# Gated mixing on two images at a time with full-width loads, and the squares moved into a forward transform whose image blocks are stationary

## The chip, the cores and the metric

One core of a Trainium2 chip runs the whole program. The metric is the device time of one execution in microseconds (us). The engines are named as the profile names them: PE is TensorE (PEld its weight loads), DVE is VectorE, ACT is ScalarE, POOL is GpSimd, SP is SyncE, which here only issues transfers. Weights stay in PE ("stationary") while the other operand streams through ("moving"). All data are float32.

## The reference, cut to what matters

The input x has 8 images, 64 channels and 256 x 256 pixels. Two layers follow each other. `_gn` normalises groups of two channels of one image.

```python
x = x + _L0_conv_ref(_gn(x), ...)     # gated mixing
x = x + _L1_conv_ref(_gn(x), ...)     # spectral layer

# layer 0, u = _gn(x), per image
y   = einsum('bwhc,dc->bwhd', u, mlp1_w) + mlp1_b
x1  = _shift1(y[..., :c]);  x2 = _shift2(y[..., c:2*c])   # quarters of the channels move by one pixel, edges repeated
x3  = sigmoid(batchnorm(u) * wbn) * u
out = bar0 * x1 + bar1 * x2          # bar from a small softmax of the pooled sums
o   = einsum('bwhc,dc->bwhd', out, mlp2_w) + mlp2_b
return o * x3

# layer 1, u = _gn(x), 64 channels in and out, m1 = m2 = 32
x_ft = rfft2(u)
out_ft[:, :, :m1, :m2]  = einsum('bixy,ioxy->boxy', x_ft[:, :, :m1, :m2],  w1)
out_ft[:, :, -m1:, :m2] = einsum('bixy,ioxy->boxy', x_ft[:, :, -m1:, :m2], w2)
return irfft2(out_ft)
```

Layer 0 comes down to four 64 x 64 matrices per image, one for each direction of shift, applied to shifted copies of x. The result is multiplied by a gate and added to x. The value that the kernel calls x1 (not the one above) is the output of layer 0.

## The kernel before

The program is a row of stages with a barrier between them. Only the third to the fifth change.

1. Statistics: x is read once in full-width tiles, DVE takes means and variances.
2. Small matrices: `wall` (the four 64 x 64 matrices of each image) and `params` (gate scale, bias, mean, offset).
3. **Gated mixing** (L511 to L740). The work is cut into 128 blocks. A block is 16 rows of one image: its upper 8 rows lie with 64 channels on partitions 0 to 63, its lower 8 rows on partitions 64 to 127, in the tile `mix_x` whose rows are W + 1 = 257 numbers long. SP loads each half with a transfer of its own (L564, L567; 9 rows of 64 channels, pieces of 1 KB). Each half must also hold the other copy, moved by one row and one column, because the matmuls take both tap pairs from one tile at a contraction of 128. So DVE copies 64 partitions up (L686) and 64 down (L691). POOL then fills the edge column with two multiplies by one, 64 partitions x 17 numbers each (L589). PE does 16 matmuls of 64 output columns and 512 moving columns (L617), two tap pairs accumulated; the two row parities write to PSUM partitions 0 to 63 and 64 to 127 and run side by side. ACT subtracts the mean (L640, in two halves of 64 partitions, in every second block one half of it on DVE, L699), takes the sigmoid (L648), issues the store (L661) and squares the output with a sum (L666). DVE adds the offset and multiplies by the gate (L721, one operand in PSUM), then adds 1, multiplies by the centred x and sums (L730, two operands in SBUF). In each turn DVE prepares block n + 2 while PE is on block n + 1. The order of each engine is written by hand: loops of 32 blocks, waits on counting semaphores.
4. A short stage between: table loads, then the second normalisation's mean and variance for all images from `sums` and `sqs` (L740 to L797).
5. **Forward transform** (L800 to L1080). x1 is read back in groups of 8 channels, image rows on the partitions. DVE adds and POOL subtracts the two halves of the image (L1007, L1077), PE transforms along the rows with the table `frow` as the stationary operand (L869, 64 output columns for the even and 64 for the odd frequencies, side by side, 512 moving), ACT evacuates (L983), PE transposes (L880), DVE evacuates (L1052) into `fwd_cols`, and PE transforms the other direction (L901) in five parts of up to 16 matmuls. The factor `ncur` of the normalisation is applied when ACT (L965) and DVE (L1023) copy the parts out.
6. Mixing of the modes, then the inverse transform, the addition of x1 and the output. These stay, but for the address from which x1 is read.

## Time and profile before

| | us |
|---|---|
| median of 3 runs | 3113.48 |
| lowest, highest | 3108.65, 3118.16 |
| the profiled execution, in all | 3114.35 |
| its span (first to last instruction) | 3112.7 |
| statistics and small matrices | 0 to 378.6 of the span |
| gated mixing and its drain | 378.6 to 1464.9 |
| second normalisation's stage | 1464.9 to 1471.9 |
| forward transform | 1471.9 to 2093.5 |
| modes, inverse, output | 2093.5 to 3112.7 |

The rows shown further down give for a group of instructions the line, the engine, the shapes, the count, the busy time and the mean of one instruction, and how long the engine was idle just before them and who ended that. A matmul in float32 has two records, so 16 matmuls are 32 records. A timeline row has a start in us from the beginning of the span and a duration.

### The profile page before, as it was taken

Reading aid. Unit: us, or ns where it says so; the run is one execution under the profiler, and the core shown is the slowest. Engines: PE = TensorE matmul, PEld = TensorE weight load, DVE = VectorE, ACT = ScalarE, POOL = GpSimd, SP = SyncE. Lnnn points to the kernel's source line nnn. Section 1 sums busy time; section 2 is a strip of 40 time slices with the busy share of each in tenths; the row PEclk is TensorE's granted clock in tenths of the full one; section 3 lists DMA queues with packets and bytes.
Section 4 is the critical chain, followed back from the end, with each engine's and each line's share of the span. In section 5 each row is a group of like instructions: output and inputs, shape, how many; then the busy total and the mean of one; then the engine's idle time right before and its main releaser. Section 6 shows DMA issues by size and latency. Waiting matters only on the chain. (4 is left out here: it accounts for less than half of the span.)

```text
span 3112.7 us, 38323 instructions
## 1 busy us (share of the span) xinstructions
PE 2255.8 (72%) x12960; PEld 1076.6 (35%) x12960; DVE 2025.2 (65%) x2317; ACT 1302.1 (42%) x1470; POOL 757.3 (24%) x477
## 2 busy tenths in 40 slices
PE   0000288888889889896899898965555989988884
PEld 0000123222223223232345444534555444444442
DVE  8999689989999999997665555640000454544442
ACT  1111078878887888886332222310001222212220
POOL 1000023222323232322655454510000111111111
PEclk9999899999999999998999999987888999998987
DMA  9999299999999999997877676739999999999999
GB/s 402 428 428 428 70 254 264 269 249 276 269 267 257 273 275 267 270 271 215 346 258 260 238 259 243 258 95 347 355 342 317 362 384 395 394 378 409 401 376 351
DMA packets 456398, 949.63 MB, mean 305 GB/s; under 512 B 16608, under 2 KB 377744, under 8 KB 410928
## 3 DMA queue, kind: packets, MB, share of 16 engines
q1 hardware_dynamic: 250720, 619.62, 61.8%
q10 hardware_dynamic: 169984, 192.95, 19.5%
q0 software_dynamic: 35536, 134.84, 11.5%
q8 instruction: 113, 1.85, 0.2%
q14 instruction: 45, 0.37, 0.0%
HBM read 653.75 MB, written 293.60 MB: 304 GB/s over the span
## 5 line engine op out<-in xcount | busy, mean ns | idle before, releaser
L617 PE MATMUL psum<-mix_x,wcur 128*64 128x512 f32 x4096 | 938.1, 614 | 148.6 <-POOL mix_x L589 137.4
L617 PEld LDWEIGHTS psum<-mix_x,wcur 128*64 128x64 f32 x4096 | 311.9, 139 | 774.2 <-issue 564.8
L1227 PE MATMUL psum<-tab_irow_icol_sign,inv_t 128*128 128x512 f32 x1024 | 497.0, 609 | 15.7 <-DVE weights_or_rows L1322 15.1
L589 POOL TENSOR_TENSOR mix_x<-mix_x,one 64x17 f32<-64x17 f32 x256 | 324.0, 1266 | 745.6 <-DVE mix_x L691 738.1
L640 ACT ACTIVATE centred<-mix_x,pcur 64x2048 f32<-64x2048 f32 x192 | 384.2, 2001 | 205.2 <-POOL mix_x L589 188.5
L1322 DVE TENSOR_TENSOR weights_or_rows<-weights_or_rows,psum 128x1024 f32<-128x1024 f32 x224 | 272.7, 1221 | 265.7 <-PE psum L1227 228.5
L983 ACT ACTIVATE fwd_rows<-psum 128x512 f32<-128x512 f32 x256 | 152.2, 598 | 414.6 <-PE psum L869 384.8
L730 DVE SCALAR_TENSOR_TENSOR mix_out<-gated,centred 128x2048 f32<-128x2048 f32 x128 | 293.6, 2294 | 39.4 <-issue 35.2
L264 DVE BATCH_NORM_STATS2 stats<-stat_x 128x6 f32<-128x512 f32 x512 | 305.4, 676 | 13.4 <-DMA stat_x<-x 13.0
L721 DVE SCALAR_TENSOR_TENSOR gated<-psum,pcur,gated 128x2048 f32<-128x2048 f32 x128 | 300.9, 2351 | 18.0 <-PE psum L617 16.4
L1052 DVE COPY fwd_cols<-psum 128x136 f32<-128x136 f32 x512 | 154.6, 394 | 237.8 <-PE psum L880 236.7
L869 PE MATMUL psum<-fwd_sum,tab_ident_frow_fcol 128*64 128x512 f32 x512 | 282.5, 635 | 28.4 <-POOL fwd_diff L1077 18.5
L1291 ACT ACTIVATE inv_t<-psum 128x256 f32<-128x256 f32 x256 | 98.4, 384 | 477.3 <-PE psum L1218 477.3
L869 PE MATMUL psum<-fwd_diff,tab_ident_frow_fcol 128*64 128x512 f32 x512 | 282.8, 636 | 0.0
L1077 POOL TENSOR_TENSOR fwd_diff<-fwd_x 128x2048 f32<-128x2048 f32 x48 | 224.3, 4673 | 239.1 <-PE psum L869 205.6
L648 ACT ACTIVATE gated<-centred,pcur 128x2048 f32<-128x2048 f32 x128 | 268.2, 2095 | 9.6 <-DVE centred L699 1.8
L1202 PE MATMUL psum<-weights_or_rows,modes_or_terms 128*16 128x64 f32 x4096 | 170.3, 354 | 135.3 <-DMA modes_or_terms<-modes_in 111.8
L1227 PEld LDWEIGHTS psum<-tab_irow_icol_sign,inv_t 128*128 128x128 f32 x1024 | 199.5, 196 | 164.8 <-issue 146.1
L666 ACT ACTIVATE square<-mix_out 128x2048 f32<-128x2048 f32 x128 | 242.4, 1894 | 3.6 <-DVE mix_out L730 3.6
L296 PE MATMUL psum<-s_ones_dmask_spread_npix,w1d 128*64 128x128 f32 x1 | 0.4, 396 | 333.7 <-PEq L200 333.7
L1218 PE MATMUL psum<-tab_irow_icol_sign,modes_or_terms 128*128 128x256 f32 x512 | 159.7, 396 | 97.1 <-ACT modes_or_terms L1285 97.1
L1334 POOL DMA_DIRECT2D out<-weights_or_rows x112 | 98.7, 886 | 463.6 <-DMA out<-weights_or_rows 229.3
(185 smaller groups left out, 1982.4 us busy)
## 6 DMA issues: line engine op xcount, KB each, us to landing
mix_x<-x SPq DMA_DIRECT2D x240, 576.0 KB, 8.0
stat_x<-x SPq DMA_DIRECT2D x64, 2048.0 KB, 13.0
x_scratch<-mix_out ACTq DMA_DIRECT2D x128, 1024.0 KB, 9.1
weights_or_rows<-x_scratch SPq DMA_DIRECT2D x112, 1024.0 KB, 10.9
out<-weights_or_rows POOLq DMA_DIRECT2D x112, 1024.0 KB, 16.5
fwd_x<-x_scratch SPq DMA_DIRECT2D x96, 1024.0 KB, 6.8
x_tile<-x_scratch SPq DMA_DIRECT2D x46, 1024.0 KB, 8.0
weights_or_rows<-L_conv_w_real SPq DMA_DIRECT2D x8, 4096.0 KB, 34.3
```

What stands on the lines that cost most here:

```text
L264: last = nc.vector.bn_stats(stats[:, at:at + 6], XT[t % NX][:, q * 512:(q + 1) * 512])
L589: last = nc.gpsimd.tensor_tensor(XT[n % NX][h, :, to], XT[n % NX][h, :, of], one[h, :], ALU.mult)
L617: last = nc.tensor.matmul(bank(k * 4 + q, 512, C, par * C), wcur[j][:, m * C:(m + 1) * C], XT[n % NX][:, r0:r0 + 3:2, m:m + W], start=(m = ...
L640: last = nc.scalar.activation(XC[n % NX][h, :].rearrange("p (r w) -> p r w", w=W), XT[n % NX][h, 1:MR:2, 1 - half:1 - half + W], ACT.Ident ...
L648: nc.scalar.activation(G[n % NX][:, :], XC[n % NX][:, :], ACT.Sigmoid, bias=pcur[j][:, 1:2], scale=pcur[j][:, 0:1]).then_inc(sig_done, 1)
L666: nc.scalar.activation(SQ[:, :], XO[k][:, :], ACT.Square, accum_out=sqs[:, bass.ds(i * NI + n, 1)]).then_inc(sq_done, 1)
L721: nc.vector.scalar_tensor_tensor(out=G[n % NX][:, :], in0=psum[:, k * SC:(k + 1) * SC], scalar=pcur[j][:, 3:4], in1=G[n % NX][:, :], op0=A ...
L730: nc.vector.scalar_tensor_tensor(out=XO[k][:, :], in0=G[n % NX][:, :], scalar=1.0, in1=XC[n % NX][:, :], op0=ALU.add, op1=ALU.mult, accum_ ...
L869: last = nc.tensor.matmul(bank(n % 2, 512, C, par * C), frow[:, par, :], ED[G0 % 2][par][:, 2 * cp:2 * cp + 2, :], start=True, stop=True)
L1077: nc.gpsimd.tensor_tensor(ED[G0 % 2][1][:, :, :], XW[G0 % NX][:, 0, :, :], XW[G0 % NX][:, 1, :, :], ALU.subtract).then_inc(diff_done, 1)
L1227: last = nc.tensor.matmul(bank(n % 2 * 2 + a), TS[n % 2][:, a * P:(a + 1) * P], icol, start=True, stop=True)
L1322: nc.vector.tensor_tensor(xw, xw, psum[:, n % 2 * 1024:n % 2 * 1024 + 1024] .rearrange("p (a k) -> p a k", a=2), ALU.add).then_inc(added, 1)
```

## The change

The mixing now takes a pair of images: the first image's 64 channels on partitions 0 to 63, the second's on 64 to 127, 8 rows a block, again 128 blocks. One transfer of 10 rows and 128 partitions fills the tile `mix_u` (U; rows of 258 numbers, six buffers). A second tile `mix_v` (V, four buffers) takes the copies: image 0's matmuls read U, image 1's read V. The sixteen matmuls keep their shape; the two images take the places of the two row parities. The loops are written out.

- POOL pads both edge columns in one instruction of 128 x 20 numbers and copies 64 partitions x 2321 numbers from U to V ("up").
- ACT copies 64 x 2322 numbers from U to V ("low"), subtracts the mean on 128 partitions, takes the sigmoid; it squares nothing here.
- DVE copies 64 x 2321 numbers inside U ("double"); both multiply steps stay, the second writes over the gate's tile, from which the store is issued (four buffers instead of two).

```diff
-            NX = 4
-            XT = [sb(ph, f"mix_x{i}", [P, MR + 1, PITCH]) for i in range(NX)]
+            NU, NV = 6, 4
+            U = [sb(ph, f"mix_u{i}", [P, OWN * PITCH]) for i in range(NU)]
+            V = [sb(ph, f"mix_v{i}", [P, TAPS * PITCH]) for i in range(NV)]
...
+                        if n >= NU:
+                            sp.wait_ge(conv_done, n - NU + 1)
...
+                        sp.dma_start(u[:, lo - r0:hi - r0, 1:W + 1],
+                                     x_rows[pair, lo:hi, :]).then_inc(loaded[n % NU], 16)
...
+                    def pad(n):
+                        pool.wait_ge(loaded[n % NU], loaded_by(n))
+                        if n >= 2:
+                            pool.wait_ge(up_done, n - 1)
...
+                    def up(n):
+                        pool.wait_ge(padded, min(n + 2, NI))
+                        if n >= NV:
+                            pool.wait_ge(conv_done, n - NV + 1)
+                        k = TAPS * PITCH - 1
+                        nc.gpsimd.tensor_copy(V[n % NV][C:P, 0:k], U[n % NU][C:P, SHIFT:SHIFT + k]).then_inc(up_done, 1)
...
+                    def low(n):
...
+                        nc.scalar.activation(V[n % NV][0:C, 0:k], U[n % NU][C:P, 0:k], ACT.Copy).then_inc(low_done, 1)
...
-                            nc.scalar.activation(SQ[:, :], XO[k][:, :], ACT.Square,
-                                                 accum_out=sqs[:, bass.ds(i * NI + n, 1)]).then_inc(sq_done, 1)
...
+                        nc.vector.tensor_copy(U[n % NU][C:P, 0:k], U[n % NU][0:C, SHIFT:SHIFT + k]).then_inc(doubled, 1)
```

The order on DVE in the middle of the mixing, before: one turn makes the upper copy of block n + 2, multiplies block n, makes the lower copy, multiplies again, and in every second turn subtracts a mean.

```order
L686 COPY mix_x3<-mix_x3 64x8x256 [waits mix_loaded3]
L719 REGISTER_ALU
L721 SCALAR_TENSOR_TENSOR gated1<-psum,pcur0,gated1 128x2048 [waits mix_sig,mix_conv]
L691 COPY mix_x3<-mix_x3 64x8x256
L727 REGISTER_ALU
L729 REGISTER_ALU [waits mix_stored1,mix_h]
L730 ISA [waits mix_sq]
L730 SCALAR_TENSOR_TENSOR mix_out1,sums<-gated1,centred1 128x2048
L699 TENSOR_SCALAR centred3<-mix_x3,pcur0 64x2048 [waits mix_doubled]
```

And in the changed kernel, two turns:

```order
L702 SCALAR_TENSOR_TENSOR gated1<-psum,pcur0,gated1 128x2048 [waits mix_sig,mix_conv]
L690 COPY mix_u3<-mix_u3 64x2321 [waits mix_v_up,mix_v_low,mix_xc]
L709 SCALAR_TENSOR_TENSOR gated1,sums<-gated1,centred1 128x2048 [waits mix_h]
L702 SCALAR_TENSOR_TENSOR gated2<-psum,pcur0,gated2 128x2048 [waits mix_sig,mix_conv]
L690 COPY mix_u4<-mix_u4 64x2321 [waits mix_v_up,mix_v_low,mix_xc]
L709 SCALAR_TENSOR_TENSOR gated2,sums<-gated2,centred2 128x2048 [waits mix_h]
```

A turn has lost one copy and the mean; the copy that is left waits for ACT's and POOL's copies instead of for the load.

POOL at the same place, before:

```order
L589 TENSOR_TENSOR mix_x0<-mix_x0,one 64x17 [waits mix_doubled]
L589 TENSOR_TENSOR mix_x0<-mix_x0,one 64x17
L586 REGISTER_ALU
L589 TENSOR_TENSOR mix_x1<-mix_x1,one 64x17 [waits mix_doubled]
L589 TENSOR_TENSOR mix_x1<-mix_x1,one 64x17
```

and in the changed kernel:

```order
L578 TENSOR_TENSOR mix_u0<-mix_u0,one 128x10x2 [waits mix_v_up,mix_loaded0]
L587 COPY mix_v1<-mix_u5 64x2321 [waits mix_conv,mix_padded]
L578 TENSOR_TENSOR mix_u1<-mix_u1,one 128x10x2 [waits mix_v_up,mix_loaded1]
L587 COPY mix_v2<-mix_u0 64x2321 [waits mix_conv,mix_padded]
L578 TENSOR_TENSOR mix_u2<-mix_u2,one 128x10x2 [waits mix_v_up,mix_loaded2]
```

The pad has moved from behind DVE's last copy to ahead of it, right behind the load, and a large copy has come to POOL.

The forward stage has no sums and differences, no transposes and nothing on POOL. A block of x1 (128 image rows x 128 columns of one channel) is the stationary operand and a table of 128 columns (33 cosines and 33 sines, each in a field of 34) is the moving one, so the result is already transposed. ACT squares each tile there with a sum, in four instructions of 128 x 1024. The second normalisation's stage is gone: the means are made at the start of the forward stage, the variance of an image when its last tile is squared (a copy `spread`, one matmul of one column, a root, two reciprocals).

```diff
-                        for par in range(2):
-                            last = nc.tensor.matmul(bank(n % 2, 512, C, par * C), frow[:, par, :],
-                                                    ED[G0 % 2][par][:, 2 * cp:2 * cp + 2, :],
-                                                    start=True, stop=True)
...
+                        for k in range(RC):
+                            for s in range(2):
+                                at = n % 2 * 1024 + k * 256 + s * P
+                                for a in range(2):
+                                    last = nc.tensor.matmul(psum[:, at:at + P],
+                                                            XW[t % NX][:, a, c0 + k, s * P:(s + 1) * P],
+                                                            frow[:, a, :], start=(a == 0), stop=(a == 1))
...
+                            nc.scalar.activation(junk[g % 2][:, :, :],
+                                                 XW[t % NX][:, :, 2 * g:2 * g + 2, :].rearrange("p a c w -> p a (c w)"),
+                                                 ACT.Square,
+                                                 accum_out=part[c % 2][:, k % GP:k % GP + 1]).then_inc(sq_done, 1)
```

PE in the forward stage before, four channels of an image:

```order
L869 MATMUL psum<-fwd_sum0,tab_ident_frow_fcol 64x512 [waits fwd_row_out]
L869 MATMUL psum<-fwd_diff0,tab_ident_frow_fcol 64x512
L880 MATMUL psum<-tab_ident_frow_fcol,fwd_rows1 128x128 [waits fwd_tr_out,fwd_row_out]
L880 MATMUL psum<-tab_ident_frow_fcol,fwd_rows1 128x128 x3
L869 MATMUL psum<-fwd_sum0,tab_ident_frow_fcol 64x512 [waits fwd_row_out]
L869 MATMUL psum<-fwd_diff0,tab_ident_frow_fcol 64x512
L880 MATMUL psum<-tab_ident_frow_fcol,fwd_rows0 128x128 [waits fwd_tr_out,fwd_row_out]
L880 MATMUL psum<-tab_ident_frow_fcol,fwd_rows0 128x128 x3
```

and in the changed kernel, eight channels with the parts of the image before between them:

```order
L796 MATMUL psum<-tab_frow_fcol_both_ident,fwd_x0 128x128 [waits fwd_row_out,fwd_loaded0]
L796 MATMUL psum<-tab_frow_fcol_both_ident,fwd_x0 128x128 x15
L808 MATMUL psum<-fwd_ones,fwd_wide 128x1 [waits norm2_spread]
L830 MATMUL psum<-tab_frow_fcol_both_ident,fwd_cols0 128x128 [waits norm2_means,fwd_row_out]
L830 MATMUL psum<-tab_frow_fcol_both_ident,fwd_cols0 128x128 x15
L796 MATMUL psum<-tab_frow_fcol_both_ident,fwd_x0 128x128 [waits fwd_row_out]
L796 MATMUL psum<-tab_frow_fcol_both_ident,fwd_x0 128x128 x15
L830 MATMUL psum<-tab_frow_fcol_both_ident,fwd_cols0 128x128 x16
```

Sixteen matmuls of 128 x 128 now stand where four of 64 x 512 and eight transposes stood, and nothing on another engine lies between the load and the first of them.

x1 in memory goes from (image, row, channel, column) to (pair, row, image of the pair, channel, column); the step from one row to the next is 128 KB instead of 64 KB, the pieces that are read stay 8 KB and those that are written 1 KB.

## Rows read from the trace of the kernel before

**Rows 1.** Busy time by stage: engines, PE clock, DMA share, GB/s; mixing, then forward.

```profile
378.60:1468.00 1089.40, 938.71 (x4103) 312.54 (x4104) 994.26 (x735) 891.87 (x578) 324.02 (x256) 0.95 1.03 263
1468.00:2086.00 618.00, 553.44 (x3150) 291.65 (x3148) 349.44 (x678) 178.51 (x321) 308.01 (x64) 0.94 0.68 244
```

**Rows 2.** Groups of instructions of the mixing: busy us, mean ns, idle before.

```profile
L617 PE MATMUL psum<-mix_x,wcur 128*64 128x512 f32 x4096 | 938.1, 614 | 148.6 <-POOL mix_x L589 137.4 <-issue 7.5 <-DVE gated L721 3.7
L640 ACT ACTIVATE centred<-mix_x,pcur 64x2048 f32<-64x2048 f32 x192 | 384.2, 2001 | 205.2 <-POOL mix_x L589 188.5 <-issue 15.7
...
L721 DVE SCALAR_TENSOR_TENSOR gated<-psum,pcur,gated 128x2048 f32<-128x2048 f32 x128 | 300.9, 2351 | 18.0 <-PE psum L617 16.4
L730 DVE SCALAR_TENSOR_TENSOR mix_out<-gated,centred 128x2048 f32<-128x2048 f32 x128 | 293.6, 2294 | 39.4 <-issue 35.2 <-DMA x_scratch<-mix_out 1.3
...
L648 ACT ACTIVATE gated<-centred,pcur 128x2048 f32<-128x2048 f32 x128 | 268.2, 2095 | 9.6 <-DVE centred L699 1.8
L666 ACT ACTIVATE square<-mix_out 128x2048 f32<-128x2048 f32 x128 | 242.4, 1894 | 3.6 <-DVE mix_out L730 3.6
...
L686 DVE COPY mix_x<-mix_x 64x2048 f32<-64x2048 f32 x128 | 156.2, 1221 | 24.4 <-DMA mix_x<-x 14.9 <-issue 5.1
...
L699 DVE TENSOR_SCALAR centred<-mix_x,pcur 64x2048 f32<-64x2048 f32 x64 | 82.4, 1287 | 2.1
```

**Rows 3.** Timeline of the mixing: start us, duration us, engine, line.

```profile
390.13 0.51 POOL L589 TENSOR_TENSOR mix_x<-mix_x,one 64x17 f32<-64x17 f32 x2 [11.62 <-DVE mix_x L691]
...
405.04 2.29 DVE L730 SCALAR_TENSOR_TENSOR mix_out<-gated,centred 128x2048 f32<-128x2048 f32 x1
405.08 3.59 POOL L589 TENSOR_TENSOR mix_x<-mix_x,one 64x17 f32<-64x17 f32 x2 [7.93 <-DVE mix_x L691]
...
407.37 1.22 DVE L686 COPY mix_x<-mix_x 64x2048 f32<-64x2048 f32 x1
...
408.73 7.11 PE L617 MATMUL psum<-mix_x,wcur 128*64 128x512 f32 x32 [2.42 <-POOL mix_x L589]
```

**Rows 4.** Timeline of the mixing, PE alone, further on.

```profile
1011.82 14.00 PE L617 MATMUL psum<-mix_x,wcur 128*64 128x512 f32 x64 [0.37 <-POOL mix_x L589]
```

**Rows 5.** Timeline of the forward stage: DVE's sum and POOL's difference.

```profile
1603.10 2.27 DVE L1007 TENSOR_TENSOR fwd_sum<-x_tile 128x2048 f32<-128x2048 f32 x1
...
1611.65 4.52 POOL L1077 TENSOR_TENSOR fwd_diff<-fwd_x 128x2048 f32<-128x2048 f32 x1 [1.83 <-PE psum L869]
...
1613.42 4.90 DVE L1007 TENSOR_TENSOR fwd_sum<-fwd_x 128x2048 f32<-128x2048 f32 x1
```

**Rows 6.** Short stretches, columns as in rows 1: loads alone, both, full-width loads.

```profile
386.00:388.00 2.00, 0.00 (x0) 0.00 (x0) 0.48 (x1) 0.00 (x0) 0.00 (x0) 0.50 1.13 216
...
964.00:966.00 2.00, 2.00 (x10) 0.69 (x12) 2.00 (x1) 1.99 (x2) 0.00 (x0) 1.00 1.09 381
...
1480.00:1490.00 10.00, 1.68 (x4) 0.59 (x6) 2.29 (x1) 0.00 (x0) 8.43 (x2) 0.50 1.01 427
```

**Rows 7.** The group of DVE's evacuation in the forward stage.

```profile
L1052 DVE COPY fwd_cols<-psum 128x136 f32<-128x136 f32 x512 | 154.6, 394 | 237.8 <-PE psum L880 236.7
```

**Rows 8.** Timeline: sixteen matmuls of the columns, and the last image's 68.

```profile
1613.80 3.83 PE L901 MATMUL psum<-tab_ident_frow_fcol,fwd_cols 128*128 128x128 f32 x32 [0.89 <-DVE fwd_cols L1052]
...
2062.76 15.58 PE L901 MATMUL psum<-tab_ident_frow_fcol,fwd_cols 128*128 128x128 f32 x136 [0.70 <-DVE fwd_cols L1052]
```

**Rows 9.** Timeline between the mixing and the forward stage.

```profile
1460.03 0.38 ACTq L661 DMA_DIRECT2D x_scratch<-mix_out  x1
...
1464.95 0.82 SPq L753 DMA_DIRECT2D tab_group_ident<-tables  x2
...
1473.64 3.37 SPq L846 DMA_DIRECT2D fwd_x<-x_scratch  x6
...
1481.43 2.29 DVE L1007 TENSOR_TENSOR fwd_sum<-fwd_x 128x2048 f32<-128x2048 f32 x1 [9.76 <-DMA fwd_x<-x_scratch]
...
1488.33 1.09 PE L869 MATMUL psum<-fwd_sum,tab_ident_frow_fcol 128*64 128x512 f32 x1 [18.53 <-POOL fwd_diff L1077]
```

More of the change, by code:

```diff
@@ L81, in constants @@
     put("spread", spread.reshape(P, -1))
+    both = np.stack([0.5 * ((p[:, None] // C == d) & (c[:, None] // 2 == c[None, :] // 2)) for d in range(2)], 1)
+    put("both", both.reshape(P, -1))
     put("sign", np.stack([np.where(p < C, 1.0, -1.0)] * 2, 1))
@@ L551, in program, with rows_of, loads_of, loaded_by @@
+            NI = NQ * NB
+            SHIFT = PITCH + 1
+            x1_out = x1.rearrange("q h e c w -> q (e c) h w")
+            def rows_of(t):
+                return t[:, :].rearrange("p (r w) -> p r w", w=PITCH)
+            def loads_of(n):
+                return 2 if n % NB in (0, NB - 1) else 1
+            def loaded_by(n):
+                return 16 * sum(loads_of(m) for m in range(n % NU, n + 1, NU))
             with nc.Block() as block:
@@ new lines, in up @@
+                    def up(n):
[4 more added lines that the diff above has]
+                        nc.gpsimd.tensor_copy(V[n % NV][C:P, 0:k], U[n % NU][C:P, SHIFT:SHIFT + k]).then_inc(up_done, 1)
+                    pad(0)
+                    for n in range(NI):
+                        if n + 1 < NI:
+                            pad(n + 1)
+                        up(n)
@@ new lines, in store @@
+                    def store(n):
+                        q, y0 = n // NB, n % NB * SP_
+                        act.wait_ge(o_done, n + 1)
+                        act.dma_start(x1_out[q:q + 1, :, y0:y0 + SP_, :].rearrange("b p r w -> (b p) r w"),
+                                      G[n % 4][:, :].rearrange("p (r w) -> p r w", w=W)).then_inc(stored[n % 4], 16)
+                    for n in range(3):
+                        centre(n)
+                        low(n)
+                    gate(0)
@@ L809, in program @@
-            RS = [sb(ph, f"fwd_rows{i}", [P, 512]) for i in range(2)]
             A = [sb(ph, f"fwd_cols{i}", [P, 2, 4 * NP, C]) for i in range(2)]
             XB = sb(ph, "fwd_modes", [C, 3, KX, M2])
+            junk = [sb(ph, f"fwd_junk{i}", [P, 2, 2 * W]) for i in range(2)]
+            part = [sb(ph, f"fwd_part{i}", [P, C // 2]) for i in range(2)]
+            wide = sb(ph, "fwd_wide", [P, 2, C // 2, 2])
+            onecol = sb(ph, "fwd_ones", [P, 1])
+            sv = sb(ph, "norm2_values", [P, 6, B])
@@ L818, in program @@
-            NR = C // 2
+            neg_done, modes_stored = sem("fwd_neg"), sem("fwd_stored")
+            n2, spread_done, sum_done, var_done, std_done, cur = (
+                sem("norm2_" + n) for n in ("means", "spread", "sum", "var", "std", "cur"))
+            recip_done = sem("norm2_recip")
+            RC = 4
+            NR = C // RC
+            GP = C // 2
             PARTS = 5
             ON_ACT, ON_DVE = (0, 2), (1, 3, 4)
-            def part_after(n):
-                g = n % NR
-                return g // 4 + 1 if g % 4 == 3 and g // 4 + 1 < PARTS else None
@@ L874, in transposes @@
[L874 to L891 removed]
+                    pe.wait_ge(tab, 64)
@@ new lines, in _ @@
+                    for b in range(B):
+                        nc.tensor.matmul(psum[0:1, 2048 + b * C:2048 + (b + 1) * C], params[0:C, b, 2:3],
+                                         ident[0:C, 0:C], start=True, stop=True)
+                    pe.wait_ge(n2, 2)
+                    for d in range(2):
+                        last = nc.tensor.matmul(bank(5 + d, NQ), both[:, d * P:(d + 1) * P], sv[:, 1, 0:NQ],
+                                                start=True, stop=True)
+                    last.then_inc(n2, 1)
@@ L990, in _ @@
-                    body(0, True)
-                    with act.Fori(1, B // 2) as i:
-                        body(i, False)
+                    for t in range(B * NG):
+                        c, g = t // NG - 1, t % NG
+                        squares(t)
+                        if c < 0:
+                            continue
+                        if g == 0:
+                            root(c)
+                        if g == 1:
+                            copies(c, 0)
+                        if g == 2:
+                            copies(c, 2)
+                        if g == 6:
+                            store(c)
@@ L1013, in take, with copies @@
                         dve.wait_ge(cur, c + 1)
-                    def copies(c, m, first=False):
-                        if m == ON_DVE[0] and not first:
+                    def copies(c, m):
+                        if m == ON_DVE[0] and c >= 1:
                             dve.wait_ge(modes_stored, c * 48)
@@ L1065, in _ @@
+                    spread(B - 1)
+                    variance(B - 1)
+                    scales(B - 1)
                     for m in ON_DVE:
```

596 lines of the change are left out of this document (242 added, 354 removed).

## Prediction

> **What bounds the kernel now.** I read the busy time by stage first [rows 1]. The mixing is the longest stage, and DVE is busy 994 of its 1089 us; PE has 939, ACT 892. In the forward stage PE is busy 553 of 618 us and DVE 349. The changed stages thus have different limits. The stages before and behind keep their instructions, and I count them at no change.
>
> *Mixing, one turn.* From the first conv (390.7 us, just behind the pad at 390.13 [rows 3]) to the last output (1460.0 [rows 9]) are 1069.3 us, or 8.35 us for each of 128 blocks. The groups of instructions [rows 2] give DVE's turn: 2.35 (L721) + 2.29 (L730) + 1.22 (L686) + the like of it (L691) + half of 1.29 (L699) = 7.73 us. ACT's turn is 1.5 x 2.00 + 2.10 + 1.89 = 7.0 us. PE needs less: two blocks without a gap take 14.00 us [rows 4], so 7.0 each. One block by itself takes 7.11 us with its drain [rows 3], so the steps inside are 14.00 - 7.11 = 6.89 us.
>
> The rest up to 8.35 is the pad. Two pads cost 0.51 us when DVE is idle, but 3.59 us when L730 begins 0.04 us ahead of them [rows 3]: the first gets through when L730 ends (407.33), the second when the copy L686 ends (408.59), and PE starts at 408.73. PE lost 137 us and ACT 189 us to this pad [rows 2]. In the forward stage it goes the other way round: DVE's sum takes 2.27 us alone and 4.90 us when it starts behind POOL's difference, which ends at 1616.17, 2.15 us before it [rows 5]. So a DVE instruction that reads two SBUF operands, or copies within SBUF, excludes one of POOL, for its whole length and in both directions. L721, with an operand in PSUM, is the one during which POOL is free.
>
> *Transfers.* Loads alone move 216 GB/s with the DMA engines fully busy; with the stores beside them, in pieces of the same 1 KB, it is 381 GB/s; full-width loads in the forward stage reach 427 [rows 6]. The low rate belongs to loads of 64 partitions, not to small pieces.
>
> **The change, part by part: mixing.**
>
> - *DVE.* One copy and the mean go. The copy that is left has 2321 numbers: 1.22 x 2321 / 2048 = 1.38 us (L686). Turn: 2.35 + 1.38 + 2.29 + 0.08 to read the sum = 6.1 us, 1.6 less. The rows only show even counts. If the odd one halves the copy's speed it costs 2.6 us and the turn 7.4.
> - *ACT.* L666 goes (1.89); the copy "low" comes, at most 2.00 x 2322 / 2048 = 2.27 us (L640); the mean is one instruction of 2.00 instead of 1.5. Turn: 2.27 + 2.00 + 2.10 = 6.4 us. The store waits for DVE's last step, and behind it on ACT stand the sigmoid, mean and copy of later blocks. They are needed one to three turns on.
> - *PE.* Same shapes, same 16 matmuls: 7.0 us a block.
> - *POOL.* The pad is one instruction of 0.25 us and no longer stands between DVE's copy and PE. The copy "up" is new, and the trace has no POOL copy. From below it is DVE's price, 1.38 us; from above POOL's two-operand subtraction, 4.52 x 2321 / 2048 = 5.1 us [rows 5]. I take half of the upper, 2.6 us, because it reads one operand instead of two. What must not overlap then is 1.38 + 2.29 + 0.25 + 2.6 = 6.5 us a turn, under 7.0. The copy can lie beside L702 (the new L721, 2.35 us). Both are released by the end of a conv, so they tend to start together.
> - *DMA.* A block moves 1280 + 1024 KB = 2.36 MB instead of 2.23. At 381 GB/s [rows 6] that is 6.2 us. With six buffers a load has five turns before it is needed.
>
> By the Trainium skill (GPSIMD Engine Reference, section 4.1 Engine selection) a one-input instruction on GpSimd runs at roughly line rate, which at its 1.2 GHz would make "up" an estimated 1.9 us and the exclusive sum 5.8 us. No row here shows it; by it the block would still be PE's 7.0 us.
>
> So PE sets the pace: 128 x 7.0 = 896 us. Before it come 1.6 us for the cold clock (as now, in the first block), behind it 4.8 us of L702 and L709. That is 902 us against 1069.3: **167 us gained**. The least is 6.89 a block, 181 us. The start stays at about 390.7: the first load is full-width and quicker, two more copies follow it.
>
> **Between the stages.** Now: last output 1460.0, stores landed 1465.0, the normalisation's tables and chain, first load issued 1473.6, landed 1481.4, and PE starts 1488.3 after POOL's difference, 28.3 us in all [rows 9]. In the changed kernel the stage between and the difference go: 5.0 + 2.5 for four tables + 7.8 for the load = 15.3 us. The new chain of means lies beside the load. **13 us gained.**
>
> **Forward stage.** From 1488.3 to the end of the last column matmul, 2062.8 + 15.6 = 2078.3, are 590.0 us [rows 8, 9]. Afterwards PE has 8 x 16 x 16 = 2048 row matmuls of 128 x 128, which have the shape of the columns' (L901). Those run at 15.58 / 136 = 0.115 us a record without a gap and 3.83 / 32 = 0.120 in the dearer place [rows 8]; two records a matmul. Rows 4096 x 0.1165 = 477 us, columns 8 x 15.6 = 125 us, cold clock some 2 us: 604 us, so **14 us lost** (2 at the lowest price, 31 at the dearest). It is all PE's. DVE's evacuation of 544 numbers is at most four of 136, 4 x 0.39 = 1.6 us [rows 7], against 3.7 us of PE for them, with two buffers. ACT's 256 squares of 1024 numbers are at most 1.89 us each, 485 us (L666 is twice as wide). They must finish for an image before PE's small matmul L808, one group after its last; ACT is ahead of PE as far as four tile buffers allow. The other instructions of the chain (variance, root, reciprocals) are released between column parts and are short.
>
> **Sum.** 3114.35 of the profiled execution (span 3112.7 and 1.65 around it; the median is 0.9 lower) - 167 - 13 + 14 = **2948 us**.
>
> **The rivals.**
>
> 1. *POOL's copy and DVE's SBUF steps take turns and pass PE.* The point is the exclusive sum 3.67 + 0.25 + copy against 7.0: from a copy of 3.1 us on it sets the block. At 3.6 us the block is 7.5 (+64 us: 3012); an odd-length copy on DVE at 2.6 us comes to the same, 7.4. For it speaks that one late copy already holds L690 and then L709; against it that POOL is free to choose the time of L702.
> 2. *Slower than before.* The same mechanism, if POOL's copy costs what its subtraction does, 5.1 us: 3.67 + 0.25 + 5.1 = 9.0 us a block, over 8.35. 128 x 2.0 = 256 us more: 3204 us. It decides from a copy of 4.4 us on, at which the mixing is as long as now. For it is that this is the only large POOL instruction in the trace; against it that it reads two operands.
> 3. *Transfers set the block.* If the 263 GB/s of the stage [rows 1] is what pieces of 1 KB allow, and not the half-width loads, 2.36 MB take 9.0 us: 3204 too. The 381 GB/s speaks against it. At a middle of 310 GB/s it is 7.6 us: 3025.
> 4. *The forward stage costs more.* If the row matmuls fall back to the clock's lower level at each tile, or loading image blocks as weights costs more than loading `fwd_cols`, say 0.13 us a record: 533 + 125, 55 us more than I count: 3003.
>
> The Trainium skill (SBUF — State Buffer, section SBUF: two separate sides) calls the ports that DVE and GpSimd share an exclusive lock, held for the whole instruction by whoever starts first. That is the mechanism of rivals 1 and 2, and the trace agrees (4.90 us instead of 2.27).
>
> **How the numbers follow.** Forecast 0.62; rival 1 0.15; rival 2 0.07; rival 3 0.07, a third of it over the old time; rival 4 0.06; the last 0.03 is mixtures near the old time. A measurement here can tell about 0.3% (9 us) from no change. Faster: 0.62 + 0.15 + 0.05 + 0.06 = 0.88 and 0.01 of the mixtures, 0.89; within 0.3% 0.02; slower 0.09. The range reaches from all parts at their least (2948 - 14 - 12 = 2922) over the lock and transfer cases to 3030; rival 2 and the worst of 3 are left out.
>
> **What would show it.** Right: in the mixing PE busy without gaps, clock 1.0, 64 records in about 14.0 us, DVE under 90% busy, POOL's copy at 2 to 3 us, over 320 GB/s; the mixing's PE time ends near 1288. In the forward stage PE records at 0.115 to 0.12 us and no wait on ACT. Wrong: PE waiting for L690, and L690 or L709 much longer than 1.4 and 2.3 us, means rival 1 or 2; DVE or POOL waiting for loads means rival 3; L796 above 0.12 us a record means rival 4. The forecast also fails if the written-out program makes the engines wait for their own instructions, which no row of this kernel prices: now some "issue" waits of 2 to 4 us each stand at its loops, 35 us ahead of L730 [rows 2].

## The result, and the profile after

| | before | after |
|---|---|---|
| median, us | 3115.82 (4 runs beside it) | 2881.18 (4 runs) |
| lowest, highest | 3108.65, 3119.55 | 2875.03, 2882.68 |
| profiled execution; its span | 3114.35; 3112.7 | 2875.03; 2873.3 |

The ratio is 0.9246, with a 95% interval of 0.9223 to 0.9268. The forecast was 2948 us with a range of 2922 to 3030: right in direction, 67 us too high, and outside the range. The stages of both traces, each from its first to its last row, show where the 239.4 us of the spans went:

| stage, us | before | after | difference | forecast |
|---|---|---|---|---|
| up to the first conv | 390.7 | 392.7 | +2.0 | 0 |
| mixing, first conv to last output | 1069.3 | 887.8 | -181.5 | -167 |
| last output to first row matmul | 28.3 | 15.0 | -13.3 | -13 |
| first row matmul to last column matmul's end | 590.0 | 586.3 | -3.7 | +14 |
| to the first load of the modes | 15.2 | 15.1 | -0.1 | 0 |
| modes | 309.8 | 289.8 | -20.0 | 0 |
| inverse and output | 709.4 | 686.6 | -22.8 | 0 |

The last two stages are the surprise: nothing in them was edited but the address of x1, and they gave 43 of the 73 us by which the profiled execution lies below the forecast (the median lies 67 below it).

**The mixing.** One long window of the kernel after and its groups of instructions (columns as in [rows 1] and [rows 2]):

```profile
400.00:1250.00 850.00, 849.65 (x3958) 282.41 (x3955) 807.79 (x511) 754.53 (x370) 442.01 (x249) 1.00 1.03 341
```

```profile
L610 PE MATMUL psum<-mix_u,wcur 128*64 128x512 f32 x2048 | 882.7, 593 | 24.5 <-DVE mix_u L690 24.5
...
L587 POOL COPY mix_v<-mix_u 64x2321 f32<-64x2321 f32 x128 | 375.2, 2931 | 10.4 <-PE psum L610 2.3
...
L709 DVE SCALAR_TENSOR_TENSOR gated<-gated,centred 128x2048 f32<-128x2048 f32 x128 | 316.8, 2475 | 4.0
...
L690 DVE COPY mix_u<-mix_u 64x2321 f32<-64x2321 f32 x128 | 219.4, 1714 | 18.4 <-ACT centred L635 12.1
```

PE is busy 849.65 of 850 us at the full clock. L610 is two groups (the other reads `mix_v`), of which this one shows all the waiting there was: 24.5 us, nearly all of it ahead of the first block, against 148.6 before [rows 2]. DVE is at 95%, and POOL's copy has a mean of 2.93 us, L709 2.48 and L690 1.71. Alone they take less. The timeline of POOL and DVE shows one copy alone at the start, and one turn in the middle where they meet:

```profile
388.93 2.12 POOL L587 COPY mix_v<-mix_u 64x2321 f32<-64x2321 f32 x1
```

```profile
804.53 3.27 POOL L587 COPY mix_v<-mix_u 64x2321 f32<-64x2321 f32 x1
```

```profile
804.45 1.36 DVE L690 COPY mix_u<-mix_u 64x2321 f32<-64x2321 f32 x1
805.85 4.10 DVE L709 SCALAR_TENSOR_TENSOR gated<-gated,centred 128x2048 f32<-128x2048 f32 x1
809.88 0.08 DVE L709 DVE_READ_ACCUMULATOR gated<-gated,centred 128x1 f32 x1
```

POOL's copy starts 0.08 us behind L690, gets through when that ends (805.81), and ends at 807.80; L709 was released at 805.85 and ends at 809.95, 2.15 us behind the copy. So the means contain each other's waiting. The two engines take turns exactly as before [rows 3, 5], but within the time that PE gives them.

How fast PE goes is read from the distance of equal records:

```profile
1271.76 0.59 PE L610 MATMUL psum<-mix_u,wcur 128*64 128x512 f32 x1
...
1275.19 0.59 PE L610 MATMUL psum<-mix_u,wcur 128*64 128x512 f32 x1
```

Eight pairs lie between these two rows: 3.43 / 8 = 0.429 us, and a block of sixteen pairs takes 6.86 us. The row's own 0.59 includes a modelled end that runs beside the next record.

**The forward stage**, the whole of it as a window, and two pieces of PE's timeline:

```profile
1295.00:1882.00 587.00, 585.03 (x5200) 582.46 (x5200) 180.12 (x252) 299.13 (x585) 0.00 (x0) 1.00 0.68 251
```

```profile
1507.45 3.74 PE L796 MATMUL psum<-tab_frow_fcol_both_ident,fwd_x 128*128 128x128 f32 x32
1511.02 3.74 PE L830 MATMUL psum<-tab_frow_fcol_both_ident,fwd_cols 128*128 128x128 f32 x32
1514.60 7.31 PE L796 MATMUL psum<-tab_frow_fcol_both_ident,fwd_x 128*128 128x128 f32 x64
```

```profile
1866.06 0.35 PE L808 MATMUL psum<-fwd_ones,fwd_wide 128*128 128x1 f32 x2 [1.30 <-DVE fwd_wide L955]
1866.27 15.55 PE L830 MATMUL psum<-tab_frow_fcol_both_ident,fwd_cols 128*128 128x128 f32 x136
```

PE and its weight loads are both busy over 99% of it, 5200 records in 585 us. From start to start 32 row records take 3.57 us and 32 column records 3.58, that is 0.112 us each; the rows' own 3.74 ends with 0.16 us of modelled tail. DVE and ACT are at 31% and 51%. The transfers run at 251 GB/s, where full-width loads reach 427 [rows 6].

**The untouched stages.** Their largest transfers, before and then after (tensors, KB of each, median us to landing):

```profile
weights_or_rows<-L_conv_w_real SPq DMA_DIRECT2D x8, 4096.0 KB, 34.3
...
out<-weights_or_rows POOLq DMA_DIRECT2D x112, 1024.0 KB, 16.5
```

```profile
out<-weights_or_rows POOLq DMA_DIRECT2D x112, 1024.0 KB, 15.3
...
weights_or_rows<-L_conv_w_real SPq DMA_DIRECT2D x8, 4096.0 KB, 31.3
```

The weights of the modes, which the change does not go near, land 3 us sooner. A window of 240 us inside the modes stage, before and after:

```profile
2125.00:2365.00 240.00, 153.68 (x3697) 145.37 (x3701) 18.96 (x14) 17.60 (x14) 0.00 (x0) 0.86 1.06 348
```

```profile
1928.00:2168.00 240.00, 169.98 (x4096) 161.27 (x4096) 21.19 (x16) 19.80 (x16) 0.00 (x0) 0.87 1.04 374
```

The DMA engines are fully busy in both, and move 348 GB/s in one and 374 in the other.

### The profile page after: what moved, and what is told of

It is laid out like the page before. It is cut to its first block and busy times, and to the rows that moved or that the text cites. A ratio compares the mean times of both kernels' runs of the same rounds, so it can differ in the third digit from the quotient of the medians.

```text
span 2873.3 us, 38693 instructions
## 1 busy us (share of the span) xinstructions
PE 2230.3 (78%) x15026; PEld 1350.6 (47%) x15026; DVE 1704.3 (59%) x1705; ACT 1317.1 (46%) x1541; POOL 576.0 (20%) x411
## 5 line engine op out<-in xcount | busy, mean ns | idle before, releaser
L610 PE MATMUL psum<-mix_u,wcur 128*64 128x512 f32 x2048 | 882.7, 593 | 24.5 <-DVE mix_u L690 24.5
L610 PE MATMUL psum<-mix_v,wcur 128*64 128x512 f32 x2048 | 882.7, 593 | 0.0
L610 PEld LDWEIGHTS psum<-mix_u,wcur 128*64 128x64 f32 x2048 | 278.4, 136 | 613.5 <-issue 605.0
L587 POOL COPY mix_v<-mix_u 64x2321 f32<-64x2321 f32 x128 | 375.2, 2931 | 10.4 <-PE psum L610 2.3
L796 PE MATMUL psum<-tab_frow_fcol_both_ident,fwd_x 128*128 128x128 f32 x3072 | 351.4, 276 | 2.4 <-DMA fwd_x<-x_scratch 2.4
L796 PEld LDWEIGHTS psum<-tab_frow_fcol_both_ident,fwd_x 128*128 128x128 f32 x3072 | 347.5, 193 | 3.7 <-DMA fwd_x<-x_scratch 2.5
L702 DVE SCALAR_TENSOR_TENSOR gated<-psum,pcur,gated 128x2048 f32<-128x2048 f32 x128 | 300.5, 2348 | 41.6 <-PE psum L610 41.3
L709 DVE SCALAR_TENSOR_TENSOR gated<-gated,centred 128x2048 f32<-128x2048 f32 x128 | 316.8, 2475 | 4.0
L610 PEld LDWEIGHTS psum<-mix_v,wcur 128*64 128x64 f32 x2048 | 278.4, 136 | 0.0
L624 ACT ACTIVATE mix_v<-mix_u 64x2322 f32<-64x2322 f32 x128 | 273.8, 2139 | 3.1
L635 ACT ACTIVATE centred<-mix_u,pcur 128x2048 f32<-128x2048 f32 x128 | 254.6, 1989 | 31.8 <-DMA mix_u<-x 31.8
L690 DVE COPY mix_u<-mix_u 64x2321 f32<-64x2321 f32 x128 | 219.4, 1714 | 18.4 <-ACT centred L635 12.1
## 6 DMA issues: line engine op xcount, KB each, us to landing
out<-weights_or_rows POOLq DMA_DIRECT2D x112, 1024.0 KB, 15.3
```

Of the source, the lines that this page charges most:

```text
L587: nc.gpsimd.tensor_copy(V[n % NV][C:P, 0:k], U[n % NU][C:P, SHIFT:SHIFT + k]).then_inc(up_done, 1)
L610: last = nc.tensor.matmul(bank(k * 4 + q, 512, C, e * C), wcur[j][:, e, m * C:(m + 1) * C], taps[e][:, r0:r0 + 2, m:m + W], start=(m == 0) ...
L624: nc.scalar.activation(V[n % NV][0:C, 0:k], U[n % NU][C:P, 0:k], ACT.Copy).then_inc(low_done, 1)
L635: nc.scalar.activation(XC[n % 4][:, :].rearrange("p (r w) -> p r w", w=W), rows_of(U[n % NU])[:, 1:SP_ + 1, 1:W + 1], ACT.Identity, bias=p ...
L702: nc.vector.scalar_tensor_tensor(out=G[n % 4][:, :], in0=psum[:, k * SC:(k + 1) * SC], scalar=pcur[j][:, 3:4], in1=G[n % 4][:, :], op0=ALU ...
L709: nc.vector.scalar_tensor_tensor(out=G[n % 4][:, :], in0=G[n % 4][:, :], scalar=1.0, in1=XC[n % 4][:, :], op0=ALU.add, op1=ALU.mult, accum ...
```

## The experiments

Each kernel is the changed one (or, where its label says so, the one before) with one edit. Stage times below are read from each run's own trace in the way of the table above. "Behind the forward transform" is modes, inverse and output together.

### Do the 43 us belong to the kernel, and to the layout of x1?

Both kernels unchanged, one profiled execution each, on one chip.

> The kernel before, once more, for its trace beside the others of this group. The stages behind the forward transform (modes, inverse, output) took 1019.2 us in the trace of before and 976.4 us in that of after, 42.8 us less, though no instruction of theirs is changed but for the address of x1. If that is a property of the kernels, this trace shows 1015 to 1023 us again (modes stage 308 to 312 us). If it is chance of one execution, it lies anywhere from 976 to 1020.

> The changed kernel, once more. If the 42.8 us are a property of the kernels, the stages behind the forward transform take 973 to 980 us again (modes 288 to 292 us). If they are chance, this trace and the one of the kernel before in this group differ by less than 15 us there, whichever way.

Measured: 3113.59 and 2877.04 us; the modes 307.0 and 291.6 us; behind the forward transform 1018.7 and 978.2 us. The difference of 40.5 us is a property of the kernels.

The third run put the image layout back:

```diff
-        x1 = nc.dram_tensor("x1_scratch", (NQ, H, 2, C, W), F32, kind="Internal").ap()
+        x1 = nc.dram_tensor("x1_scratch", (B, H, C, W), F32, kind="Internal").ap()
...
+                        for e in range(2):
+                            act.dma_start(x1_out[2 * q + e:2 * q + e + 1, :, y0:y0 + SP_, :]...,
+                                          G[n % 4][e * C:(e + 1) * C, :]...)
```

> The changed kernel with x1 in memory as before, (image, row, channel, column), 64 KB from row to row; each store is therefore two transfers of 64 partitions. Theory 'layout': the 23 us gained in the inverse and output come from the pair layout, so they are given back: 2875 + 23 = 2898 us, up to 2918 if the modes stage goes with it. Theory 'not the layout': behind the forward transform 973 to 980 us, in all 2870 to 2885 us. The mixing should stay at 6.86 us a block in either, as the stores have slack.

Measured: 2882.86 us (ratio to before 0.926, 0.9244 to 0.9275); modes 292.7, inverse and output 686.8, together 979.5 us. The layout has nothing to do with it. The mixing stayed at 889.7 us.

### The place of the tiles in SBUF

The change made four small tiles smaller or dropped them (`wall` by 512 bytes a partition, `params` by 16, which take 32 of room, `sqs` 512, `norm2` 64), and with that moved every large tile behind them by 1120 bytes. Before, they begin at 24416 bytes, 96 past a multiple of 256; after, at 23296, a multiple of 256. An unused tile moves them alone:

```diff
         mrow = sb(top, "mrow", [1, B * C])
+        pad = sb(top, "pad", [P, 8])     # 32 bytes; 32, 64 or 40 numbers in the other runs
```

> The changed kernel with an unused tile of 32 bytes a partition ahead of the large tiles. In the changed kernel the tiles into which the stages behind the forward transform load begin at multiples of 64 bytes in SBUF, in the kernel before 32 bytes off such a multiple; this run puts them 32 bytes off again. Theory 'alignment': modes, inverse and output go from 976 back to some 1016 us, in all 2910 to 2925 us. Theory 'something else' (place of a tensor in DRAM, layout): 2875 to 2883 us as without the edit.

> The kernel before with the same unused 32 bytes, which puts its large tiles at multiples of 128 bytes. Theory 'alignment': modes 290 instead of 307 to 310 us, modes, inverse and output together some 976 instead of 1019 us, in all 3065 to 3080 us, with the mixing as it was. Theory 'something else': 3110 to 3116 us.

> The changed kernel with an unused tile of 256 bytes a partition, so that the large tiles begin at multiples of 512 bytes instead of 256. If only the 64 bytes matter, 2875 to 2883 us, no change. If a coarser step matters too, the stages behind the forward transform fall below 970 us.

> The changed kernel with an unused tile of 128 bytes a partition: the large tiles begin 128 bytes off a multiple of 256 (in the changed kernel they are at multiples of 256, with 256 bytes more at multiples of 512, and both take 290 to 293 us for the modes). Theory '64 or 128 bytes are the step': modes 290 to 293, behind the forward transform 976 to 979 us, as without the edit. Theory '256 bytes are the step', which would explain why the kernel before gained nothing from 128: modes 307 to 314, behind the forward transform 1015 to 1025 us.

> The kernel before with an unused tile of 160 bytes a partition, which puts its large tiles at multiples of 512 bytes. Theory '256 bytes are the step': behind the forward transform 976 to 985 instead of 1019 us, in all 3068 to 3080 us. Theory 'it is not the start of the tiles alone' (a tensor's place in DRAM, the image layout of x1 together with it): 1015 to 1020 us there, in all 3105 to 3116 us.

| run | large tiles begin, past a multiple of 256 bytes | modes | inverse and output | whole, us | ratio to before, 95% |
|---|---|---|---|---|---|
| after | 0 | 289.8 | 686.6 | 2881.18 | 0.9223 to 0.9268 |
| `e4_after_512` | 0 | 292.5 | 685.7 | 2877.70 | 0.9239 to 0.9279 |
| `e4_after_shift32` | 32 | 313.7 | 710.7 | 2926.06 | 0.9395 to 0.9428 |
| `e6_after_shift128` | 128 | 309.0 | 707.4 | 2917.16 (one run) | |
| before | 96 | 309.8 | 709.4 | 3115.82 | 1 |
| `e4_before_aligned` | 128 | 307.8 | 709.9 | 3106.15 | 0.9968 to 0.9998 |
| `e6_before_256` | 0 | 288.3 | 686.8 | 3072.82 | 0.9845 to 0.9919 |

My first form of the theory, that multiples of 64 or 128 bytes are enough, gave 3065 to 3080 us for `e4_before_aligned` and fell. Multiples of 256 fit all seven. The same windows of 240 us in the modes stage, first the changed kernel moved by 32 bytes, then the kernel before moved to a multiple of 256:

```profile
1933.00:2173.00 240.00, 149.22 (x3584) 140.36 (x3584) 19.72 (x14) 18.16 (x14) 0.00 (x0) 0.85 1.06 344
```

```profile
2124.00:2364.00 240.00, 169.99 (x4096) 162.40 (x4096) 21.17 (x16) 19.93 (x16) 0.00 (x0) 0.88 1.04 374
```

The changed kernel falls to 344 GB/s, about the rate of the one before (348), and the one before rises to that of the changed one, 374, with the same 4096 records in the window. So the cause is shown in both directions: in these stages the transfers are the bound, and in the modes stage, where most pieces are of 1 KB, they go 6 to 9% faster when the tiles begin at a multiple of 256 bytes in SBUF. The inverse and output gain 3%.

The records of single transfers by the DMA engines tell the two stages apart. In the modes stage the queue that ACT issues on carries 32768 records of 1 KB, all of them loads of weights into SBUF. Their mean is 51.0 to 51.5 ns in the four kernels that are off a multiple of 256 and 46.4 to 46.5 ns in the three that are on one. In the last stage x1 is loaded in records of 8 KB (332 to 336 ns off, 325 on) and the output is stored in records of 4 KB (172 to 173 ns off, 167 to 168 on). Loads of 8 KB pieces in the forward stage land in 6.8 us in the changed kernel and 6.9 us with either shift.

The Trainium skill (DMA: Bandwidth & Descriptors, section How a descriptor splits into AXI transactions) says that a piece is carried in transactions of 256 bytes that must begin at multiples of 256, and that one which starts elsewhere fetches from the boundary below; it words this for reading. For 1 KB that makes an estimated five transactions instead of four. The trace agrees with the step of 256 and with the sign. The page also counts 32-byte beats, by which 32 bytes off would cost least and 128 most (an estimated 33 and 36 instead of 32); here 32 bytes off gave 344 GB/s and 128 bytes off 352, so the number of beats is not what decides. That the extra transaction is the reason is not shown; the runs show the step.

### Do POOL's copy and DVE's steps add up?

```diff
                         nc.gpsimd.tensor_copy(V[n % NV][C:P, 0:k], U[n % NU][C:P, SHIFT:SHIFT + k]).then_inc(up_once, 1)
+                        pool.wait_ge(up_once, n + 1)
+                        nc.gpsimd.tensor_copy(V[n % NV][C:P, 0:k], U[n % NU][C:P, SHIFT:SHIFT + k]).then_inc(up_done, 1)
```

> The changed kernel, but POOL makes each copy 'up' twice (2 x 2.12 us, its least duration in the trace of after). Theory 'the lock adds up': DVE's copy 1.36 + its multiply 2.29 + pad 0.23 + 4.24 = 8.1 us a turn that must not overlap, over PE's 6.86; the mixing grows by 128 x 1.26 = 161 us, to some 3040 us in all, PE waits for DVE's copy L690. Theory 'POOL has room': its turn of 4.5 us is under 6.86 and nothing changes, 2875 to 2890 us.

Measured: 3006.50 us (ratio 0.9649 to 0.9686), the mixing 1011.9 instead of 887.8 us. PE waited for DVE's copy (L690, line 692 of this kernel) as the lock's theory said; "POOL has room", at most 2890 us, is out by 116 us. The size was 124 us instead of 161. The timeline of DVE, a whole turn:

```profile
817.92 2.35 DVE L704 SCALAR_TENSOR_TENSOR gated<-psum,pcur,gated 128x2048 f32<-128x2048 f32 x1
820.30 1.36 DVE L692 COPY mix_u<-mix_u 64x2321 f32<-64x2321 f32 x1
821.70 4.09 DVE L711 SCALAR_TENSOR_TENSOR gated<-gated,centred 128x2048 f32<-128x2048 f32 x1
825.72 0.08 DVE L711 DVE_READ_ACCUMULATOR gated<-gated,centred 128x1 f32 x1
825.72 2.34 DVE L704 SCALAR_TENSOR_TENSOR gated<-psum,pcur,gated 128x2048 f32<-128x2048 f32 x1
```

POOL in the same turn:

```profile
818.15 2.12 POOL L587 COPY mix_v<-mix_u 64x2321 f32<-64x2321 f32 x1
820.34 3.31 POOL L589 COPY mix_v<-mix_u 64x2321 f32<-64x2321 f32 x1
823.99 1.90 POOL L578 TENSOR_TENSOR mix_u<-mix_u,one 128x20 f32<-128x20 f32 x1 [0.34 <-DMA mix_u<-x]
```

The first copy lies beside L704 (line 702 of the changed kernel), which reads PSUM, and neither is longer than alone. The second starts just behind L692 and holds L711 in its turn, and the pad then waits for L711.

The turn is 825.72 - 817.92 = 7.80 us, and DVE is "busy" all of it: 1.80 us of L711 (line 709 of the changed kernel) are waiting for POOL's second copy. The exclusive steps, added at their durations alone, are 8.1 us; they turn round in 7.8. A sum of exclusive durations is thus right to some 4% here, from above: as the turn is shorter than the sum, the recorded durations exclude each other for nearly, but not quite, their whole length.

### Is POOL the right place for the copy?

```diff
-                        nc.gpsimd.tensor_copy(V[n % NV][C:P, 0:k], U[n % NU][C:P, SHIFT:SHIFT + k]).then_inc(up_done, 1)
...
+                        nc.vector.tensor_copy(V[n % NV][C:P, 0:k], U[n % NU][C:P, SHIFT:SHIFT + k]).then_inc(up_done, 1)
```

> The changed kernel with the copy 'up' on DVE instead of POOL. POOL keeps only the pad, so the lock costs almost nothing, but DVE's turn is 2.35 + 1.36 + 1.36 + 2.29 + 0.08 = 7.44 us and a bit, over PE's 6.86. Theory 'the copy is free on POOL because of the time of L702': the mixing grows by 128 x 0.6 to 0.7 = 77 to 90 us, in all 2955 to 2965 us. Theory 'the lock was costing DVE as much as the copy' (L709 and L690 are 0.5 us above their least as it is): 2875 to 2900 us.

Measured: 2945.11 us (ratio 0.9429 to 0.9487), the mixing 952.5 us, 64.7 more, where the first theory had 77 to 90. DVE's turn became the bound:

```profile
898.39 2.35 DVE L698 SCALAR_TENSOR_TENSOR gated<-psum,pcur,gated 128x2048 f32<-128x2048 f32 x1
900.77 1.37 DVE L684 COPY mix_v<-mix_u 64x2321 f32<-64x2321 f32 x1
902.17 1.36 DVE L686 COPY mix_u<-mix_u 64x2321 f32<-64x2321 f32 x1
903.57 2.29 DVE L705 SCALAR_TENSOR_TENSOR gated<-gated,centred 128x2048 f32<-128x2048 f32 x1
905.79 0.08 DVE L705 DVE_READ_ACCUMULATOR gated<-gated,centred 128x1 f32 x1
905.79 2.35 DVE L698 SCALAR_TENSOR_TENSOR gated<-psum,pcur,gated 128x2048 f32<-128x2048 f32 x1
```

7.40 us a turn, 0.54 over PE's 6.86, and no row is longer than it is alone. The copy on POOL makes two DVE rows longer on average (0.35 and 0.19 us over their least), and is still the cheaper place: it can lie beside L702 (2.35 us a turn), as the first copy of the run above does, and what must not overlap stays under PE's turn.

### Does the width of the loads matter?

```diff
+                        for e in range(2):
+                            h = slice(e * C, (e + 1) * C)
+                            sp.dma_start(u[h, lo - r0:hi - r0, 1:W + 1],
+                                         x_rows[q * P + e * C:q * P + (e + 1) * C, lo:hi, :]
```

> The changed kernel, but each load of the mixing is two transfers of 64 partitions, as in the kernel before. Theory 'half-width transfers are slow only when they stand alone': with the stores beside them 2.36 MB a block go at some 381 GB/s, 6.2 us under PE's 6.86, and nothing changes, 2875 to 2890 us. Theory 'the width of the loads set the mixing before': at the 263 to 275 GB/s of the mixing before a block takes 8.6 to 9.0 us, PE waits through POOL's pad for loads, in all 3100 to 3150 us.

Measured: 2879.40 us (ratio 0.9219 to 0.9275), the same as with full width. The first load alone, before any store, is the one place with a difference; first this kernel, then the changed one, in the same two microseconds:

```profile
386.00:388.00 2.00, 0.00 (x0) 0.00 (x0) 0.00 (x0) 0.85 (x1) 0.23 (x1) 0.50 1.13 210
```

```profile
386.00:388.00 2.00, 0.00 (x0) 0.00 (x0) 0.00 (x0) 1.98 (x2) 0.00 (x0) 0.50 1.09 348
```

210 against 348 GB/s, so the low rate of [rows 6] does belong to loads of 64 partitions alone; it costs 4.9 us once (the first conv starts at 397.59 instead of 392.69). With stores beside them the half-width loads move 345 GB/s (900 to 950 us), as much as is asked for. Full-width loading, which gave the change part of its name, is worth nothing in the middle of this stage.

### What sets a record of the row matmuls?

```diff
-                                    last = nc.tensor.matmul(psum[:, at:at + P], ..., frow[:, a, :], ...)
+                                    last = nc.tensor.matmul(psum[:, at:at + 2 * NM2], ..., frow[:, a, 0:2 * NM2], ...)
```

> The changed kernel, but the row matmuls (L796) stream only the 68 columns of the table that are used instead of 128; everything else as it is. Theory 'columns set the record': 0.1115 x 68 / 128 = 0.059 us a record, rows 243 instead of 457 us; then the loads set the stage, 134 MB at some 427 GB/s = 314 us plus the last columns, and the forward stage falls from 586 to about 390 us, in all some 2680 us. Theory 'the weight load sets the record' (two loads of 128 rows a matmul, PE's load slot 49.7 of 50 us busy): records stay at 0.11 us, the stage at 570 to 590 us, in all 2860 to 2880 us.

Measured: 2936.26 us (ratio 0.9418 to 0.945), slower by 55 us, which neither theory had. Two windows of its forward stage:

```profile
1296.00:1412.00 116.00, 116.00 (x546) 116.00 (x545) 17.66 (x18) 39.05 (x73) 0.00 (x0) 0.50 0.50 191
1450.00:1900.00 450.00, 450.00 (x4016) 448.31 (x4014) 141.06 (x201) 227.11 (x446) 0.00 (x0) 1.00 0.70 258
```

In the second, 4016 records take 450 us, 0.112 each: with about half the moving columns the record takes as long as with 128. So with 68 columns they are not what sets it, and of the two theories the weight load is the one left. PEld is busy 448.31 of the 450 us, and the one-column matmul L808 in the changed kernel needs 0.21 us for its two records, 0.105 each (from 1866.06 to 1866.27 above). No run changed the number of stationary columns, so a fixed cost of a record is not excluded. With 128 moving columns the two sides are about even, by an estimate from the mixing: a record of 512 columns takes 0.429 us, and a quarter of that is 0.107. In the first window the granted clock was 0.50, that is 1.2 GHz, for 116 us, though PE streamed row matmuls without a gap, at 116 / 546 = 0.212 us a record. It rose while the first column matmuls ran:

```profile
1404.69 7.03 PE L796 MATMUL psum<-tab_frow_fcol_both_ident,fwd_x 128*128 128x68 f32 x32
1411.52 0.53 PE L808 MATMUL psum<-fwd_ones,fwd_wide 128*128 128x1 f32 x2
1411.90 5.00 PE L830 MATMUL psum<-tab_frow_fcol_both_ident,fwd_cols 128*128 128x128 f32 x32
1416.74 3.46 PE L796 MATMUL psum<-tab_frow_fcol_both_ident,fwd_x 128*128 128x68 f32 x30
```

and stayed up afterwards; why it stayed down for so long, no run shows. In the changed kernel the mean clock of 1295 to 1300 us is 0.63 already, and 1.00 from there on:

```profile
1295.00:1300.00 5.00, 4.50 (x26) 4.51 (x27) 0.00 (x0) 4.27 (x8) 0.00 (x0) 0.63 1.01 428
1300.00:1350.00 50.00, 50.00 (x450) 50.00 (x449) 15.62 (x14) 35.44 (x65) 0.00 (x0) 1.00 0.87 341
```

All four runs of the kernel with 68 columns have a mean clock of 0.931 to 0.933 against 0.951 or 0.952, so this was not the chance of one execution. The loss follows from it: 546 x (0.212 - 0.112) = 55 us.

The Trainium skill (TensorE: Matmul & The Clock Gate, section LDWEIGHTS (loading the stationary operand)) gives a weight load of P columns as P / 1.2 ns, by which 128 columns take an estimated 107 ns. The records of 112 ns, with 68 moving columns and with 128, agree with it to 5%.

## Why the prediction was wrong, point by point

**What failed first: "The stages before and behind keep their instructions, and I count them at no change."** It missed 43 us of the 73, the largest part of the error. The instructions are kept, but the places of their tiles are not, since all stages stack on the same small tiles: the 1 KB records of the weights' loads went from 51.5 to 46.4 ns. The profile of before already showed the DMA engines busy to the full there, so that any change in the cost of a piece would be seen in the time. Without this the changed kernel takes 2917 to 2926 us (`e6_after_shift128`, `e4_after_shift32`), about the lower end of the range, and the kernel before with its tiles at multiples of 256 takes 3073. Some 1.2 to 1.5% of the 7.5% is therefore the accident of place, and the rest is the change itself.

**Mixing: mechanism right, block mis-sized.** PE without gaps at full clock, DVE at 95% (I had said under 90; the waits for POOL count as busy, and its steps alone are 6.1 of 6.86 us, 89%), POOL's copy between 2 and 3 us, 341 GB/s: all as described. The term "7.0 us a block" measured 6.86. It was half the duration 14.00 of a row of 64 records [rows 4], and such a row ends with the modelled tail of its last record: at 0.429 us a pair the 32 pairs take 13.7 us. 128 x 0.14 = 18 us less. Of 887.8 us, 128 x 6.86 = 878 and 4.8 for L702 and L709 leave 5, where I had 1.6: the first block takes 9.3 us up to the start of the next, 2.4 more than the others, and the blocks behind it have a mean distance of 6.88 through short waits. Together 14.5 us. The first conv came 2.0 us later than I had counted. My "least", 6.89, was the better number, and I gave it only to the range.

**DVE and POOL.** The odd count did not slow DVE's copy (1.36 us alone; 1.38 forecast). POOL's copy was taken at 2.6 us, half of the subtraction's price; alone it is 2.12. The Trainium skill's rule (GPSIMD Engine Reference, section 4.1 Engine selection), an estimated 1.9 us, was nearer. Rival 1's mechanism is real, and its size is now known: the copy doubled costs 124 us. With one copy of 2.12 the exclusive steps are 6.0 us and stay under PE's 6.86. Of its two signs one came without the other: single rows of L709 do take 4.10 us, and PE does not wait. Rival 2 fell with the same number.

**Transfers, rival 3.** 2.36 MB a block at 341 GB/s is what 6.86 us ask for, and PE waits for none of it. The half-width run shows that the 263 GB/s of before was what the slower blocks asked for, and no limit.

**Between the stages:** 15.3 us forecast, 15.0 measured.

**Forward stage: sign wrong, by the same mistake in the reading.** Rows were counted at 0.1165 us a record, a middle of 15.58 / 136 and 3.83 / 32 [rows 8], durations over counts again. The shorter row has the greater share of tail, and so looked like a "dearer place" that does not exist. From start to start a record takes 0.112: rows 4096 x 0.112 = 459 us instead of 477, the seven images' columns that lie inside 7 x 136 x 0.112 = 107, the last one's 15.6, 122 instead of 125. What is left of the 586.3 is 5 us (the cold clock, 1.30 of waiting for `fwd_wide`, and the eight small matmuls L808 of some 0.21 us each), where I had 2. That is the 18 us. The lower end of the range had a slip as well: at the lowest price, 15.58 / 136, rows and columns come to 594 us, 4 more than 590.0 and not 2, or 6 more with the cold clock, which puts that end at 2924 to 2926 us. Rival 4 fell: 128 moving columns did not let the clock drop, and loading image blocks costs what loading `fwd_cols` does.

**The written-out program** did not make PE wait for its instructions. L709's idle time before it is 4.0 us in all, where L730 had 35.2 us of "issue" [rows 2].

## What to carry to other kernels

Where a stage is set by transfers of pieces around 1 KB, look up at which address in SBUF its tiles begin: 256-byte multiples were worth 6 to 9% of the rate in the modes stage here, and an edit elsewhere can give or take them. When a rate is taken from a row of many pipelined matmuls, use the distance between starts, not duration over count: the tail made 2% of a block of the mixing and 4% of a row of 32 records. Before narrowing the moving side of a matmul, see whether PEld is as busy as PE; where it was, here, nothing was gained, and 55 us were lost through the clock.

## What the hardware did that I had not expected

- 1 KB pieces from tiles that begin 32, 96 or 128 bytes past a multiple of 256: 344, 348 and 352 GB/s; at the multiple: 374. That whole stages differ by 20 to 24 us with no edit in them was not in any row that I had read for the prediction.
- A gapless stream of matmuls with 68 moving columns was granted 1.2 GHz for 116 us, where the same stream with 128 columns had 2.4 within 5 us.
- DVE and POOL report the time in which they wait for each other as busy: L711's 2.29 us became 4.09, with no releaser in the row. Only the least duration of a group tells its own cost.
- Loads of 1 KB into SBUF pay for the address themselves: their records are 51 to 52 ns off a multiple of 256 and 46 on one. What stays open is whether stores out of SBUF pay too: in the last stage loads and stores are both some 3% shorter, they share the DMA engines, and the runs moved all large tiles together. Nor was it tried what the mixing's own pieces, which begin 4 bytes into a row, would gain, as PE hides them.
